# Second rotary attention of an eight-block decoder kernel: who expands the keys, and where its first queries and scores stand

## The chip, the cores and the metric

The kernel is one program on one core of a Trainium2 chip. The metric is the device time in microseconds of one execution, the median of several. The core's engines work from queues of their own: TensorE (PE) for matrix products, VectorE (DVE), ScalarE (ACT), GpSimd (POOL) for elementwise work, and SyncE (SP), which here issues the transfers. They wait for each other by semaphores that the program counts by hand. Fp32 products take two passes over TensorE, so a product of 128x128 by 128x512 appears as two matmuls. TensorE's clock is granted at 1.2 or 2.4 GHz; the profile gives the granted share (PEclk, 1.00 is 2.4 GHz).

## What is computed

x has 16 sequences of 64 tokens with 128 features (1024 tokens). Four pairs of blocks are added to it, each block behind a layer norm and scaled by tanh of a gate:

```
x = x + tanh(g_xattn[0]) * L0_xattn(layernorm(x), ctx)        # a running sum with decay
x = x + tanh(g_ffn[0])   * L0_ffn(layernorm(x))               # 8 experts, 512 hidden
x = x + tanh(g_xattn[1]) * L1_xattn(layernorm(x), ctx)        # first rotary attention
x = x + tanh(g_ffn[1])   * L1_ffn(layernorm(x))               # 8 gated experts, 352 hidden
x = x + tanh(g_xattn[2]) * L2_xattn(layernorm(x), ctx)        # additive attention over all pairs
x = x + tanh(g_ffn[2])   * L2_ffn(layernorm(x))               # 16 gated experts, 128 hidden, top 4
x = x + tanh(g_xattn[3]) * L3_xattn(layernorm(x), ctx, ctx)   # second rotary attention
x = x + tanh(g_ffn[3])   * L3_ffn(layernorm(x))               # 8 + 1 experts, 512 hidden
```

The second rotary attention, which the change is mostly about:

```
Q = (q @ W_q.T).reshape(B, T_q, 16, 8).transpose(0, 2, 1, 3)   # K, V alike from ctx
Q = apply_rope(Q, cos_q, sin_q)
K = apply_rope(K, cos_k, sin_k)
attn = softmax(einsum('bhqd,bhkd->bhqk', Q, K) / sqrt(8))
out = einsum('bhqk,bhkd->bhqd', attn, V) @ W_o.T
```

## The kernel before

All activations lie transposed: features on the 128 partitions, the 1024 tokens as columns in two halves, t = 0 and 1. The program has one function per engine; within it every block is written in the order in which the engine is to do it. What follows are the names that the change and the prediction use.

**Layer norms** have a number j (0 to 7, two per pair of blocks) and a half t. TensorE makes the centred x (`norm_mean`, L442), ScalarE squares it (`norm_square`, L872) and copies it to `xc` (`norm_copy`, L875), TensorE sums the squares (`norm_var`, L449, matmuls with one column), VectorE adds epsilon (`norm_eps`, L1191), GpSimd takes the power -1/2 (`norm_power`, L1688), TensorE spreads it over the partitions (`norm_spread`, L459), and VectorE multiplies (`norm_out`, L1196). `LNBANK` names the PSUM banks of mean, variance and spread. In the MoE blocks `norm_high` and `norm_low` split the result in two for products of three passes.

**Pair sums** (additive attention). For each of 32 groups g VectorE (even g) or GpSimd (odd g) adds features and text to a tile of 2048 columns, ScalarE takes its tanh (L1025) and TensorE sums it with weights (L651). Between the groups stands work for the next block, chosen by `if g == ...` on each engine: norm 5 of the first half, and the key products of the second rotary attention (`prepare_keys`, L490).

**Third MoE** (m.layer 2, 16 experts, 32 steps; step s is expert s % 16 of half s // 16). For each step TensorE makes the two up products (L695 to L697), ScalarE applies silu (`hidden`, L1055), VectorE multiplies both (`product`, L1468, called by `ahead()`), VectorE scales by the token's gate (`scale`, L1476 for steps 0 to 3 with the gate from PSUM, L1480 later with the gate from `g_half`), and TensorE adds the down product (`down`, L712, a plain fp32 product). Up products run 14 steps ahead of down products, so behind step 17 only down products are left. The routing of each half (top experts, weights) is a row of small VectorE instructions, with `ahead()` and norm steps put between them by the lists `first` and `second`. The up weights are split in high and low parts by ScalarE (L920) and GpSimd (`low_up2`, L1704). The down weights of experts 0 to 7 lie in `work[:, 2T:3T]`.

**Rotary attention** (i = 0 and 1) works on 8 pairs of sequences p. `queries(t)` makes two products (L526, L527) from the norm's output; VectorE rotates them (`rotate`, L1208 to L1210) and writes the rows masked for one half of the heads (L1230), ScalarE those of the other (L960). The keys stand rotated in `kT` and are expanded with a mask to 4 copies in `kexp`, which is `work[:, 0:4T]` (`expand_keys`, GpSimd, L1709, four instructions, the last two after the third MoE's step 23, because the down weights lie in their place). Then `scores(p)` (L544), VectorE's maximum and subtraction (`soft`, L1236 and L1240), ScalarE's exponential (L969), TensorE's transposes (`turn`, L554), ScalarE's copies (L978), the values product (L569), VectorE's division (L1248, L1251), `turn_out` and `project`. The first values product writes banks in which the second half's queries stand, and waits for their rotation.

SyncE loads weights into `w_f32`, which has two slots of 1024 columns for the last MoE; each load waits until the split parts of the weights that lay there are made.

## Time and profile before

| | us |
|---|---|
| runs of the kernel | 623.39, 623.45, 624.53 |
| median | 623.45 |
| the profiled execution | 623.69 |
| its span, first to last instruction | 621.9 |
| mean granted clock of TensorE | 0.98 |
| busy: TensorE, VectorE, ScalarE, GpSimd | 568.1, 452.2, 410.7, 125.8 |

The profile is of one execution. Its times count from the first instruction; the 1.8 us between span and execution lie around it. The blocks follow each other: pair sums to 359 us, third MoE to 468, second rotary attention to 510, last MoE to the end. An engine's timeline gives start, duration, engine, source line, operation, output and inputs; the bracket at the end is the idle time in front of the instruction and what ended it. A matmul row's duration can be longer than its share of the engine, since matmuls are pipelined: the distance between starts tells the price. The view of the chain follows the work that ended last back through the engines.

### The profile page before, as it was taken

The page shows a single profiled execution, that of the slowest core. Times are in us where ns is not written, and L with a number is a line of the kernel's source. Part 1 is how long each engine was busy: PE and PEld are TensorE (multiplying, and loading weights), DVE is VectorE, ACT ScalarE, POOL GpSimd, SP SyncE. Part 2 cuts the span into 40 slices and gives each one's busy share as a digit, 9 for nine tenths or more (in the row PEclk, how much of TensorE's full clock was granted, in tenths as well). Part 3 has the DMA queues.
Part 4 walks back from the last instruction along what each step waited for, and adds up shares of the span by engine and source line. Part 5 has one row for each costly group of instructions (what it writes and reads, how often), then busy time and mean ns, then how long its engine had stood idle before and what let it go on. Part 6 is the DMA issues. An engine that isn't in the chain of part 4 may idle for free.

```text
span 621.9 us, 8752 instructions
## 1 busy us (share of the span) xinstructions
PE 568.1 (91%) x3282; PEld 393.1 (63%) x3282; DVE 452.2 (73%) x684; ACT 410.7 (66%) x573; POOL 125.8 (20%) x78
## 2 busy tenths in 40 slices
PE   7999999989998999997866889899978999999997
PEld 5667887747676777774211357466535767688886
DVE  4358988778565898887878486756677946687786
ACT  4779888828654566657999875422303765988885
POOL 5400000332200000005999622200060210000000
PEclk9999999989998999998999899999998999999999
DMA  6217210101102521020000040605600110721100
...
DMA packets 16782, 40.27 MB, mean 65 GB/s; under 512 B 1834, under 2 KB 6058, under 8 KB 16740
## 3 DMA queue, kind: packets, MB, share of 16 engines
...
HBM read 39.01 MB, written 0.70 MB: 64 GB/s over the span
## 4 chain that ended last, share of the span: by engine, by line
PE 68%; DVE 16%; ACT 12%; issue 3%; POOL 1%; DVEq 0%; ACTq 0%; POOLq 0%
PE ps L669 38%; ACT work L1025 7%; PE ps L712 4%; DVE h_lo L1491 3%; PE ps L569 2%; PE ps L695 2%; PE ps L442 2%; PE ps L544 2%; PE ps L697 2%; PE ps L696 2%; PE ps L459 2%; PE ps L449 2%; PE ps L554 1%; PE ps L651 1%; PE ps L436 1%
## 5 line engine op out<-in xcount | busy, mean ns | idle before, releaser
L1491 DVE TENSOR_TENSOR h_lo<-h_act,h_hi 128x512 fp32r<-128x512 f32 (+1 forms) x136 | 120.0, 886 | 41.0 <-ACT h_hi L1062 40.4
L669 PE MATMUL ps<-n_hi,w_hi 128*128 128x512 f32 (+1 forms) x232 | 86.2, 405 | 6.8 <-DVE h_act L1468 4.3
L1062 ACT CAST h_hi<-h_act 128x1024 fp32r<-128x1024 f32 (+1 forms) x88 | 75.3, 856 | 15.3 <-PE ps L669 12.8
L669 PE MATMUL ps<-n_hi,w_lo 128*128 128x512 f32 (+1 forms) x232 | 83.6, 394 | 0.0
L669 PE MATMUL ps<-n_lo,w_hi 128*128 128x512 f32 (+1 forms) x232 | 83.3, 393 | 0.0
L1688 POOL TENSOR_TENSOR rstd<-var_eps,minus_half 128x4 f32<-128x4 f32 x16 | 17.8, 1114 | 315.0 <-DVE var_eps L1191 315.0
L669 PE MATMUL ps<-h_hi,w_hi 128*128 128x512 f32 (+1 forms) x184 | 65.9, 400 | 4.5 <-DVE h_lo L1491 4.3
L669 PE MATMUL ps<-h_hi,w_lo 128*128 128x512 f32 (+1 forms) x184 | 64.5, 393 | 0.0
L669 PE MATMUL ps<-h_lo,w_hi 128*128 128x512 f32 (+1 forms) x184 | 64.4, 392 | 0.0
L1025 ACT ACTIVATE work<-work,p_rest 128x2048 f32<-128x2048 f32 x32 | 61.5, 2000 | 2.0 <-DVE work L1356 2.0
L1722 POOL TENSOR_TENSOR work<-xc,txt 128x2048 f32<-128x2048 f32 x16 | 58.3, 3683 | 5.0 <-ACT xc L1002 4.3
L1055 ACT ACTIVATE h_act<-ps 128x512 f32<-128x512 f32 (+1 forms) x48 | 28.6, 596 | 41.2 <-PE ps L669 41.2
L651 PE MATMUL ps<-work,p_rest 128*32 128x512 f32 x256 | 37.0, 637 | 20.1 <-ACT work L1025 20.1
L669 PEld LDWEIGHTS ps<-n_hi,w_hi 128*128 128x128 f32 (+1 forms) x232 | 42.7, 185 | 19.9 <-DVE h_act L1468 5.4
L669 PEld LDWEIGHTS ps<-n_hi,w_lo 128*128 128x128 f32 (+1 forms) x232 | 42.9, 185 | 10.6
L669 PEld LDWEIGHTS ps<-n_lo,w_hi 128*128 128x128 f32 (+1 forms) x232 | 43.1, 186 | 10.1 <-issue 0.5
L1468 DVE SCALAR_TENSOR_TENSOR h_act<-ps,h_act 128x512 f32<-128x512 f32 (+1 forms) x48 | 32.9, 686 | 20.6 <-ACT h_act L1055 20.5
L669 PEld LDWEIGHTS ps<-h_hi,w_hi 128*128 128x128 f32 (+1 forms) x184 | 34.5, 189 | 15.5 <-DVE h_lo L1491 8.0
L1048 ACT ACTIVATE h_act<-ps,p_attn 128x512 f32<-128x512 f32 (+1 forms) x44 | 38.7, 880 | 4.9 <-PE ps L669 4.4
L1356 DVE TENSOR_TENSOR work<-ps,txt 128x2048 f32<-128x2048 f32 x16 | 36.3, 2282 | 7.3 <-ACT xc L1002 5.2
L1048 ACT ACTIVATE h_act<-ps 128x1024 f32<-128x1024 f32 (+1 forms) x44 | 38.1, 866 | 4.5 <-PE ps L669 4.5
L669 PEld LDWEIGHTS ps<-h_hi,w_lo 128*128 128x128 f32 (+1 forms) x184 | 34.8, 189 | 7.6
...
## 6 DMA issues: line engine op xcount, KB each, us to landing
...
```

What stands on the lines that cost most here:

```text
L651: mm = pe.matmul(ps[32 * q:32 * q + 32, DOTS[g // B]], l2pad[:, 31 - g:63 - g], pairs[:, g % 6, q * 512:(q + 1) * 512], start=(g % B == 0) ...
L669: mm = pe.matmul(dst[i], wap(wt, e, lo, size, rows), mv[i], start=(first and c == 0), stop=(last and c == 2))
L712: pe.matmul(ps[:, acc + t], down2(e), h_part[step % 16], start=False, stop=(step + 1 == m.last_of(t))).then_inc(s["h_used"], 1)
L1025: act.activation(pairs[:, g % 6], pairs[:, g % 6], ACT.Tanh, bias=l2b[:, 0:1]).then_inc(x2["tanh"], 1)
L1048: act.activation(places(h_act, m, step), src, ACT.Gelu, **kw).then_inc(s["act"], 1)
L1055: act.activation(h_part[step % parts][0:size], ps[0:size, 2 * (step % 2)], ACT.Silu, **kw).then_inc(s["act"], 1)
L1062: act.copy(places(h_hi, m, step), places(h_act, m, step)).then_inc(s["hi"], 1)
L1356: dve.tensor_tensor(*sum_of(g, ps[:, FEAT[g // B]]), ALU.add).then_inc(x2["sumA"], 1)
L1468: dve.scalar_tensor_tensor(h, ps[0:size, 2 * sl + 1], b3, h, ALU.add, ALU.mult).then_inc(s["mul"], 1)
L1491: dve.tensor_tensor(lo, src, hi.bitcast(F32), ALU.subtract).then_inc(s["lo"], 1)
L1688: pool.tensor_tensor(rstd[:, r], var_eps[:, r], minus_half[:, r], ALU.pow).then_inc(ln["rstd"], 1)
L1722: pool.tensor_tensor(*sum_of(g, xc[:, half(g // B)]), ALU.add).then_inc(x2["sumB"], 1)
```

## The change

It has five parts.

1. The keys of the second rotary attention are expanded by ScalarE instead of GpSimd, in eight activations of 128x8x64, two behind each of the steps 23, 24, 28 and 29 of the third MoE. GpSimd expands only the keys of the first. The down weights 0 to 7 move from `work` to the second half of `w_f32`, so that `kexp`'s place is free; SyncE loads them once the low parts of the up weights 0 to 7 are made, and the last MoE's second load waits for step 23's down product.
2. The second attention's queries of the first half are made behind down product 28, rotated before the MoE's last sum into x; its first scores stand directly behind the last down product, with the second half's norm around scores 0 and 1.
3. In both attentions the second half's queries stand behind the transposes of pair 0. Norm 2's and 6's second half use banks 6 and 7.
4. In the third MoE `norm_out(5, 1)` is followed by a product, and scale 0 and 1 stand inside the second half's routing.
5. Norm 5's first half is moved by one sum in the pair sums.

The diff, with what the prediction speaks of:

```diff
-        LNBANK.update({(5, 1): (5, 7, 5), (6, 0): (6, 7, 6), (6, 1): (5, 7, 5)})
+        LNBANK.update({(5, 1): (5, 7, 5), (2, 1): (6, 7, 6), (6, 0): (6, 7, 6), (6, 1): (6, 7, 6)})
...
-            return cols(work[:, 2 * T:3 * T] if e < 8 else diag, e, P)
+            return cols(w_f32[:, 8 * P:16 * P] if e < 8 else diag, e, P)
...
                     load_up2(2)
-                    load_down2(0)
                     load_up2(3)
                     sp.wait_ge(x2["bc"], 4)
                     load_down2(1)
+                    low_ready(sp, m, 7, "u")
+                    load_down2(0)
...
                 for e in range(m.slots):
+                    if m.layer == 3 and e == 1:
+                        sp.wait_ge(mo[2]["h_used"], MOES[2].index(7, 1)[0] + 1)
                     load(m, e)
...
+                if i == 0:
+                    queries(0, 0)
+                    norm_mean(2, 1)
+                    norm_var(2, 1)
+                    scores(0, 0)
+                    norm_spread(2, 1)
+                    scores(0, 1)
+                else:
+                    scores(1, 0)
+                    norm_mean(6, 1)
+                    scores(1, 1)
+                    norm_var(6, 1)
+                    keep_busy(2, 4)
+                    norm_spread(6, 1)
                 for p in range(PAIRS):
                     turn(p)
+                    if p == 0:
+                        queries(i, 1)
                     if p + 2 < PAIRS:
-                        scores(p + 2)
+                        scores(i, p + 2)
...
-                    if g in (26, 28):
-                        prepare_keys(1, 0, (g - 26) // 2)
-                    if g == 29:
+                    if g in (26, 29):
+                        prepare_keys(1, 0, (g - 26) // 3)
+                    if g == 28:
                         norm_var(5, 0)
-                    if g == 31:
+                    if g == 30:
                         norm_spread(5, 0)
...
-            moe(MOES[2], {19: [lambda: norm_mean(6, 0)], 21: [lambda: norm_var(6, 0)], 24: [lambda: norm_spread(6, 0)]})
+            moe(MOES[2], {19: [lambda: norm_mean(6, 0)], 21: [lambda: norm_var(6, 0)], 24: [lambda: norm_spread(6, 0)], 28: [lambda: queries(1, 0)]})
...
+            def expand_keys(t, h):
+
+                act.wait_ge(pre["k"], 2 + t + 1)
+                low_ready(act, MOES[2], 15, "u")
+                src = kT[1][:, half(t)].rearrange("p (b k) -> p b k", k=S)
+                ins = act.activation(kexp[:, 8 * t:8 * t + 8, h], src, ACT.Copy, scale=hmask[:, h:h + 1])
+                if h == 3:
+                    ins.then_inc(at["kexp"], 2)
...
-                    if g == 29:
+                    if g == 28:
                         norm_square(5, 0)
                         norm_copy(5, 0)
...
+                        for t in range(2):
+                            if step - 23 - 5 * t in (0, 1):
+                                for h in range(2):
+                                    expand_keys(t, 2 * (step - 23 - 5 * t) + h)
                     load_table(ACT.Exp)
                     norm_square(6, 0)
                     norm_copy(6, 0)
+                    query_rows(1, 0)
                     return
...
+                if i == 0:
+                    query_rows(0, 0)
+                    norm_eps(2, 1)
+                    soft(0)
+                    norm_out(2, 1)
+                    soft(1)
+                else:
+                    soft(0)
+                    norm_eps(6, 1)
+                    soft(1)
+                    norm_out(6, 1)
+                query_rows(i, 1)
...
-                    first = iter([ahead, rest, lambda: norm_eps(5, 1), ahead, rest, lambda: norm_out(5, 1), lambda: norm_low(5, 1), ahead])
+                    first = iter([ahead, rest, lambda: norm_eps(5, 1), ahead, rest, lambda: (norm_out(5, 1), ahead()), lambda: norm_low(5, 1), ahead])
...
-                    for _ in range(3):
+                    for _ in range(2):
                         ahead()
-                    second = iter(6 * [ahead] + 2 * [rest])
+                    second = iter(4 * [ahead] + [lambda t=t: (ahead(), scale(t)) for t in range(2)] + 2 * [rest])
...
+                    query_rows(1, 0)
                     add(1)
                     return
...
-            pool.wait_ge(pre["k"], 4)
-            for q in range(2):
-                expand_keys(1, q)
-            pool.wait_ge(mo[2]["h_used"], MOES[2].index(7, 1)[0] + 1)
-            for q in range(2, 4):
-                expand_keys(1, q)
             norm_power(6, 1)
```

How it moves instructions on the engines. TensorE from the third MoE's last down products (outputs from `vblk`) to the second attention's transposes and first values product, before and, with the line numbers of the changed kernel, after:

```order
L712 MATMUL ps<-vblk,diag 128x512 x4
L526 MATMUL ps<-n,p_rest 128x512
L527 MATMUL ps<-n,p_rest 128x512
L442 MATMUL ps<-x,p_first 128x512
L449 MATMUL ps<-var_w,sq 128x1 x4
L544 MATMUL ps<-work 64x256 x8
L459 MATMUL ps<-p_first,rstd 128x128 x4
L544 MATMUL ps<-work 64x256 x8
L526 MATMUL ps<-n,p_rest 128x512
L527 MATMUL ps<-n,p_rest 128x512
L554 MATMUL ps<-p_first,y_g 128x128 x8
```

```order
L723 MATMUL ps<-vblk,diag 128x512
L528 MATMUL ps<-n,p_rest 128x512
L529 MATMUL ps<-n,p_rest 128x512
L723 MATMUL ps<-vblk,diag 128x512 x3
L544 MATMUL ps<-work 64x256 x8
L445 MATMUL ps<-x,p_first 128x512
L544 MATMUL ps<-work 64x256 x8
L452 MATMUL ps<-var_w,sq 128x1 x4
L439 MATMUL ps<-warm 128x512 x2
L462 MATMUL ps<-p_first,rstd 128x128 x4
L558 MATMUL ps<-p_first,y_g 128x128 x8
L528 MATMUL ps<-n,p_rest 128x512
```

The first half's queries (outputs from n) moved in front of three down products, the scores (from `work`) in front of the mean (from x), and the second half's queries behind the transposes (from `y_g`).

ScalarE in the third MoE's second half, from the activations of steps 20 to 23 (`y_g`) to the table load behind step 31:

```order
L1055 ACTIVATE y_g<-ps,p_rest 128x512 x4
L1055 ACTIVATE txt<-ps,p_rest 128x512 x2
L1055 ACTIVATE kT<-ps,p_rest 128x512 x2
L1055 ACTIVATE vblk<-ps,p_rest 128x512 x4
L892 ACT_TABLE_LOAD
```

```order
L1076 ACTIVATE y_g<-ps,p_rest 128x512 x4
L965 ACTIVATE work<-kT,p_attn 128x8x64 x2
L1076 ACTIVATE txt<-ps,p_rest 128x512
L965 ACTIVATE work<-kT,p_attn 128x8x64 x2
L1076 ACTIVATE txt<-ps,p_rest 128x512
L1076 ACTIVATE kT<-ps,p_rest 128x512 x2
L1076 ACTIVATE vblk<-ps,p_rest 128x512
L965 ACTIVATE work<-kT,p_attn 128x8x64 x2
L1076 ACTIVATE vblk<-ps,p_rest 128x512
L965 ACTIVATE work<-kT,p_attn 128x8x64 x2
L1076 ACTIVATE vblk<-ps,p_rest 128x512 x2
L903 ACT_TABLE_LOAD
```

Four pairs of expansions (into `work`) stand between the activations.

VectorE at the end of the second half's routing in the third MoE (`rt_` tiles), with products (L1468, then L1500) and scalings (L1476, then L1508):

```order
L1376 SCALAR_TENSOR_TENSOR rt_equal<-rt_rank,rt_equal 128x64
L1377 TENSOR_TENSOR rt_chosen<-rt_above,rt_equal 128x64
L1418 TENSOR_TENSOR rt_w<-rt_e,rt_chosen 128x64
L1421 TENSOR_REDUCE rt_m<-rt_w 128x4
L1422 RECIPROCAL rt_m<-rt_m 128x4
L1424 TENSOR_SCALAR rt_m<-rt_m,p_first 128x4
L1425 TENSOR_TENSOR rt_w<-rt_w,rt_m 128x64
L1476 TENSOR_TENSOR h_act<-h_act,ps 128x512 x2
L1468 SCALAR_TENSOR_TENSOR vblk<-ps,p_rest,vblk 128x512
```

```order
L1508 TENSOR_TENSOR h_act<-h_act,ps 128x512
L1408 SCALAR_TENSOR_TENSOR rt_equal<-rt_rank,rt_equal 128x64
L1409 TENSOR_TENSOR rt_chosen<-rt_above,rt_equal 128x64
L1450 TENSOR_TENSOR rt_w<-rt_e,rt_chosen 128x64
L1453 TENSOR_REDUCE rt_m<-rt_w 128x4
L1454 RECIPROCAL rt_m<-rt_m 128x4
L1456 TENSOR_SCALAR rt_m<-rt_m,p_first 128x4
L1457 TENSOR_TENSOR rt_w<-rt_w,rt_m 128x64
L1500 SCALAR_TENSOR_TENSOR vblk<-ps,p_rest,vblk 128x512
```

The two scalings behind the routing are gone from there; the second of them is the first row of the piece after.

## Rows read from the trace of the kernel before

**Rows 1.** the page's busy times, first line: busy us, share, instructions

```profile
PE 568.1 (91%) x3282; PEld 393.1 (63%) x3282; DVE 452.2 (73%) x684; ACT 410.7 (66%) x573; POOL 125.8 (20%) x78
```

**Rows 2.** timeline of the last pair sums: start, us, engine, line, operation, idle before

```profile
350.11 5.79 ACT L1025 ACTIVATE work<-work,p_rest 128x2048 f32<-128x2048 f32 x3
...
350.31 1.05 PE L449 MATMUL ps<-var_w,sq 128*128 128x1 f32 x8
...
352.17 1.06 PE L651 MATMUL ps<-work,p_rest 128*32 128x512 f32 x8 [0.81 <-ACT work L1025]
...
355.81 2.02 PE L459 MATMUL ps<-p_first,rstd 128*128 128x128 f32 x8
...
357.76 1.06 PE L651 MATMUL ps<-work,p_rest 128*32 128x512 f32 x8
```

**Rows 3.** timeline of the first routing in the third MoE

```profile
381.99 0.75 DVE L1468 SCALAR_TENSOR_TENSOR y_g<-ps,p_rest,y_g 128x512 f32<-128x512 f32 x1
...
382.89 0.47 PE L695 MATMUL ps<-n_hi,w_hi 128*128 128x512 f32 x1 [1.35 <-DVE y_g L1468]
...
384.35 0.60 PE L736 MATMUL ps<-p_first,rt_w 128*16 128x128 f32 x4
```

**Rows 4.** timeline of the second routing's end and the first down product

```profile
401.85 1.28 DVE L1476 TENSOR_TENSOR h_act<-h_act,ps 128x512 f32<-128x512 f32 x2
...
402.67 1.10 PE L712 MATMUL ps<-h_act,work 128*128 128x512 f32 x2 [2.12 <-DVE h_act L1476]
```

**Rows 5.** timeline of the last down products and GpSimd's expansion

```profile
447.45 1.12 PE L712 MATMUL ps<-h_act,work 128*128 128x512 f32 x2 [0.45 <-DVE h_act L1480]
...
453.59 9.02 POOL L1709 TENSOR_TENSOR work<-kT,p_attn 128x1024 f32<-128x1024 f32 x4
...
453.87 2.38 DVE L1480 TENSOR_TENSOR kT<-kT,work 128x512 f32<-128x512 f32 x1
...
456.18 0.67 DVE L1196 TENSOR_TENSOR n<-xc,ps 128x512 f32<-128x512 f32 x1
...
458.48 5.88 DVE L1480 TENSOR_TENSOR vblk<-vblk,work 128x512 f32<-128x512 f32 x4
...
463.21 4.54 PE L712 MATMUL ps<-vblk,diag 128*128 128x512 f32 x6 [1.17 <-DVE vblk L1480]
```

**Rows 6.** one line's instructions, 400 to 468 us: ns min/median/max, first and last start

```profile
L1480 DVE TENSOR_TENSOR y_g<-y_g,work x8: 681/684/693, 411.3 to 452.1; 128x512 f32<-128x512 f32 x8
```

**Rows 7.** timeline: ScalarE's last activation there, and its query copy

```profile
445.33 0.69 ACT L1055 ACTIVATE vblk<-ps,p_rest 128x512 f32<-128x512 f32 x1 [1.55 <-PE ps L697]
...
471.56 0.72 ACT L960 ACTIVATE work<-xc,p_attn 128x512 f32<-128x512 f32 x1
```

**Rows 8.** windows: PE, PEld, DVE, ACT, POOL busy, then PEclk

```profile
463.00:468.00 5.00, 4.79 (x7) 2.03 (x8) 1.57 (x4) 0.00 (x0) 0.00 (x0) 0.66 0.00 0
473.00:478.00 5.00, 5.00 (x37) 2.84 (x29) 3.83 (x4) 1.06 (x1) 0.35 (x1) 0.66 0.01 3
```

**Rows 9.** the chain that ended last, 444 to 484 us: start, us, engine, line

```profile
467.75 0.86 PE ps L526 x2
...
472.38 1.09 PE ps L544 x16
...
477.21 1.24 DVE mx L1236
...
478.47 1.22 DVE work L1240
...
480.93 0.70 DVE xc L1210
```

**Rows 10.** timeline: where the second attention's first values product starts

```profile
481.72 1.11 PE L569 MATMUL ps<-vblk,g_sb 128*64 128x18 f32 x32 [0.76 <-issue]
```

**Rows 11.** timeline of the first attention: first transposes, second half's query rotation

```profile
138.69 1.04 PE L554 MATMUL ps<-p_first,y_g 128*128 128x128 f32 x8
...
139.13 0.74 DVE L1208 SCALAR_TENSOR_TENSOR xc<-ps,p_attn 128x512 f32<-128x512 f32 x1
```

91 lines of the change are left out of this document (40 added, 51 removed).

## The prediction

> **What bounds the kernel now.** I read the page's busy times first: TensorE works for 568.1 of 621.9 us [rows 1], so time can be won only where TensorE pauses or runs at half clock, and a step moved on another engine pays only if TensorE waits for it. The waits of TensorE between 340 and 484 us then give four places. (a) The pair sums end with a norm's variance, spread and last sum in a row, though ScalarE's last tanh is over at 355.90 [rows 2]. (b) The first half's routing holds back one product [rows 3]. (c) The first down product waits 2.12 us for the gate scaling behind the second routing [rows 4]. (d) The last down products wait for VectorE, whose scalings stretch while GpSimd expands the keys [rows 5], and behind them stands the start of the second attention [rows 9, 10]. Everywhere between (c) and (d) TensorE is dense, and the rest of the second attention and the last MoE follow (d) unchanged, so what is won here should arrive at the end whole.
>
> The sum is made against the profiled execution, 623.69 us (span 621.9 and 1.8 outside it). That is 0.24 above the median of the runs, 623.45.
>
> **(a) Norm of the third MoE's first half.** Moved: variance before sum 28 instead of 29, spread before sum 30 instead of 31, the second key product into the gap, ScalarE's square and copy ahead of its tanh 28. ScalarE: the same instructions in another order; tanh 31 still ends near 355.9 [rows 2]. VectorE's and GpSimd's rstd then follow VectorE's sum 30 and GpSimd's sum 31 as now, and are ready some 2 us before the spread needs them. TensorE's last sum now ends at 357.76+1.06=358.82, because the spread (2.02) sits between tanh 31 and it. After: the spread fills the wait before sum 30, and sum 31 starts some 0.1 us behind tanh 31, at 356.0, and ends near 357.1. Gain 358.8-357.1 = **1.7**, which both the softmax on VectorE and the copies on ScalarE pass on. Low end 0.3: if the half clock, under which the spread took 2.02 for 8 small matmuls, comes now too, the filled gap is slower by the same amount. High end 2.0. I take 1.7, since the key product now fills the stretch in which TensorE twice waited 0.8 us.
>
> **(b) Product 4 pulled ahead of norm_low.** TensorE waited 1.35 us for it [rows 3]. Without that wait it stands at the transposition of the gates, for which VectorE needs the same steps as before; that now starts at 384.35. VectorE does the same instructions up to the gates, in another order and without idling, so the gates come hardly earlier, at about 384.0. Gain 1.35 at first, **0.35** behind the gates; ends 0 and 1.0.
>
> **(c) Scale 0 and 1 inside the second routing.** scale 0 now runs behind product 12, near 399.4, so the first down product no longer waits: **2.1** [rows 4]. Cost: 2 x 0.64 us (1.28 for two) more VectorE time before the gates of the second half and product 14, which starts near 403.4 instead of 403.0. The up product that needs it starts three pieces of TensorE work later, after 405, so nothing waits. Ends 1.5 and 2.2.
>
> **(d1) Keys expanded by ScalarE.** GpSimd's four expansions take 9.02 us. In exactly that stretch VectorE's scalings (both inputs in SBUF) take 2.38 and on average 5.88/4=1.47 us, where the same line elsewhere has a median of 0.684 [rows 5, 6]; a norm multiplication that reads PSUM stays at 0.67 in the same stretch. So it is GpSimd that stretches them. Without it the tail is TensorE's own: from 447.45 on 13 down products of 0.86, the norm's mean 0.86 and spread 0.86, variance about 0.8, two query products of 0.86 (price in [rows 9]): 17 x 0.86 + 0.8 = 15.4, plus 0.4 of small waits which the stretch up to 456.4 already had, so the last down product ends at 463.3 with the queries already done, against 467.7 now without them [rows 5]. This includes the end of the half clock of [rows 8], in which the last three down products took 4.54 instead of 2.6.
> ScalarE pays: 8 activations of 512 elements a partition, two behind each of steps 23, 24, 28 and 29. It has 1.55 us idle before each activation there; nearest price is the query copy, also from SBUF with a mask as scale, 0.72 [rows 7]. 2 x 0.72 = 1.44 < 1.55: free. The far bound is the slowest 512-element instruction of that stretch, VectorE's 2.38 [rows 5]; at that they would not be free (rival R4). I take 0.72, the same engine and the same form.
>
> **(d2) Start of the second attention.** Queries of the first half run between down products, so VectorE's rotation (three of 0.70) starts at about 460.9 and its mask copy (0.5) ends at 463.4, just as the last down product ends. Scores 0 at 463.7 for 1.09; softmax pair 0 of 1.24 + 1.22 ends at 467.4 [rows 9]; softmax pair 1 beside the second half's variance, rstd and spread until 470.1; norm_out 0.67 until 470.9; transposes of pair 0 done meanwhile; queries 1.72; rotation 2.1; first values product at 475.1. Now it starts at 481.72 [rows 10]. Gain **6.6** for d1 and d2 together at full clock. What pauses again: TensorE waits about 0.5, 1.1 and 1.2 us in this start, and two stretches with such pauses before were followed by half clock (0.66 on average over 463 to 468 and 473 to 478, [rows 8]). I count one such stretch: of the spread and the second half's queries, 0.86+1.72 us of work, about half is doubled, which takes **1.2** back. So d = 5.4; ends 4.0 and 6.8.
>
> **(e) First attention.** The same function puts the second half's queries behind the first transposes. Here nothing else is won: the queries, which ran from 136.9, now wait for the exponential of pair 0 (to 137.3) and the transposes of 1.04 us, so they come 1.4 us later. VectorE, busy with softmax pair 1 until 139.1, hides 0.3 of that; its rotation starts near 140.2 instead of 139.13 [rows 11], and pair 2's softmax and the first output stand behind it. **1.0 lost**; ends 1.3 and 0. The other bank for that half's norm costs nothing: mean and spread share a bank before and after.
>
> **(f) At no cost.** The down weights 0 to 7 go to a free slot of w_f32 after GpSimd's eighth low part (about 373 us) instead of at 359, are needed at 400. On SP the slot makes the last MoE's second load wait for step 23's down product (about 453); behind it on SP stand only loads that wait for splits after 488, and ScalarE reads that slot near 490. If that cover is gone, it would be the transfer's 4 us.
>
> Sum: -1.7 -0.35 -2.1 -5.4 +1.0 = -8.55. 623.69 - 8.55 = 615.1; in the median's frame 614.9, rounded to **615.0**.
>
> **Rivals.** R1: no half clock in the new start; +1.2 won: 613.8. For it: the first attention has the same pauses and kept full clock. R2: half clock also at the end of the pair sums; 1.4 less: 616.4. For it: TensorE works no more there than now. R1 and R2 differ only in the clock. The trace shows it fall to 1.2 GHz after short pauses with work between them. The Trainium skill (TensorE: Matmul & The Clock Gate, HAM oscillation) also tells of kernels where micro-idles alone make the clock swing; by it R2 is the case. R3: the expansion does not stretch the scalings, something else there does; then the tail stays as now and d keeps only the moved queries, about 2: 618.5. Against it: the same line is never slow outside. R4, slower: ScalarE's expansions hold up the up products of the third MoE. ScalarE has 2.25 us a step with 0.69 of its own and TensorE some 1.2 us of slack; each of four steps with two expansions of X delays by 2X+0.69-2.25. At 2.38 each that is 4 x 3.2 - 2.4 = 10.4 lost: 625.4. It decides against the change from X near 2.15, where the loss reaches 8.5. Against it: the 0.72 of [rows 7].
>
> **Chances.** Forecast (614.3 to 615.9) 0.45; R1 0.20; R2 0.16; R3 or another half of d missing 0.10; R4 0.04; a small wait not seen, up to 2 us, 0.05. The range 612.2 to 618.5 leaves out R4, the end of R3, and the sum of all high ends. A measurement of this kernel can tell about 0.2% from no change. Faster by over that: 0.94; same 0.02; slower 0.04.
>
> **What would show it.** (a) last pair sum ends under 1.3 us behind the last tanh. (c) No wait before the first down product. (d) No scaling over 0.8 us; From the start of the down product that waits 0.45 us for its scaling (447.45 now) the last one ends after 15.8 us instead of 20.3, the first scores start within 0.6 us of that, and the first values product starts after 27.7 us (28.9 with one half clock) instead of 34.3. (e) Values product 0 of the first attention 1 us later. Half clock in other stretches than assumed, or ScalarE late at step 24 or 29, would make it wrong.

## The result, and the profile after

The changed kernel takes **614.03 us** (median of four runs, 613.25 to 616.97); the kernel before, run beside it, 623.87 us (623.39 to 624.53). The ratio is 0.9843, with a 95% interval of 0.9804 to 0.9881: faster by 1.6%. The forecast was 615.0, the range 612.2 to 618.5. The profiled execution of the changed kernel took 613.41 us, its span is 611.6 (before 623.69 and 621.9), and its mean granted clock is 0.988 (before 0.980).

The page of the changed kernel, busy times; beside [rows 1] TensorE works 4.6 us less and its pauses are 5.7 us shorter:

```profile
PE 563.5 (92%) x3281; PEld 390.9 (64%) x3284; DVE 445.4 (73%) x684; ACT 415.8 (68%) x581; POOL 117.0 (19%) x74
```

The stretch that the change is about. TensorE of the changed kernel from the last down products on (start, duration, then engine, line, operation, tiles, count, and in brackets the wait and who ended it):

```profile
443.61 1.13 PE L723 MATMUL ps<-h_act,w_f 128*128 128x512 f32 x2 [0.45 <-DVE h_act L1512]
...
455.10 1.02 PE L528 MATMUL ps<-n,p_rest 128*128 128x512 f32 x2
455.96 1.02 PE L529 MATMUL ps<-n,p_rest 128*128 128x512 f32 x2
456.82 2.74 PE L723 MATMUL ps<-vblk,diag 128*128 128x512 f32 x6
459.89 1.09 PE L544 MATMUL ps<-work 64*64 64x256 f32 x16 [0.34 <-DVE work L1253]
...
465.39 1.16 PE L462 MATMUL ps<-p_first,rstd 128*128 128x128 f32 x8 [0.89 <-POOL rstd L1721]
...
467.33 1.12 PE L528 MATMUL ps<-n,p_rest 128*128 128x512 f32 x2
...
471.47 1.11 PE L573 MATMUL ps<-vblk,g_sb 128*64 128x18 f32 x32 [1.14 <-issue]
```

The down product at 443.61 is the one of [rows 5] that stood at 447.45. From it to the end of the last down product it is now 15.8 us (456.82 and three times 0.86 make 459.4), with the queries L528 and L529 of the first half already among them; before it was 20.3. The first scores L544 start at 459.89, 0.5 us behind that end and after a wait of 0.34, and the first values product L573 starts 27.9 us behind the down product at 443.61; in [rows 10] it was 34.3. No half clock is left in this piece (columns: window, its length, busy time of each engine, then the granted clock ahead of the DMA share; [rows 8] are the windows of before):

```profile
456.00:465.00 9.00, 8.09 (x52) 3.72 (x51) 6.52 (x9) 2.85 (x4) 0.67 (x1) 1.00 0.01 2
465.00:474.00 9.00, 7.47 (x84) 5.25 (x88) 6.79 (x9) 3.54 (x6) 0.34 (x1) 1.00 0.00 0
```

VectorE's gate scalings are now all alike; the minimum, median and maximum stand in ns, and the line is L1512. In [rows 5] the one on kT took 2.38 us and those on vblk 1.47:

```profile
L1512 DVE TENSOR_TENSOR vblk<-vblk,work x8: 678/682/686, 427.2 to 454.9; 128x512 f32<-128x512 f32 x8
...
L1512 DVE TENSOR_TENSOR kT<-kT,work x4: 681/683/686, 421.4 to 452.5; 128x512 f32<-128x512 f32 x4
```

ScalarE's expansions, two at a time (L965), between its activations L1076. Two take 1.32 us together, and 0.34 us are left before the next activation, where [rows 7] had 1.55:

```profile
424.10 1.32 ACT L965 ACTIVATE work<-kT,p_attn 128x512 f32<-128x512 f32 x2
425.76 0.69 ACT L1076 ACTIVATE txt<-ps,p_rest 128x512 f32<-128x512 f32 x1 [0.34 <-PE ps L708]
```

The end of the pair sums, TensorE. The last sum ends at 358.04, 2.0 us behind ScalarE's last tanh (356.01); in [rows 2] it ended at 358.82, 2.9 us behind it:

```profile
351.56 2.08 PE L493 MATMUL ps<-ctxT,p_rest 128*128 128x512 f32 x2
353.56 1.54 PE L662 MATMUL ps<-work,p_rest 128*32 128x512 f32 x8
355.04 1.16 PE L462 MATMUL ps<-p_first,rstd 128*128 128x128 f32 x8
356.12 1.92 PE L662 MATMUL ps<-work,p_rest 128*32 128x512 f32 x16
```

and the start of the first attention, where the values product L573 stood at 141.31 before:

```profile
132.73 1.98 PE L544 MATMUL ps<-work 64*64 64x256 f32 x16 [0.44 <-DVE work L1253]
134.64 1.85 PE L462 MATMUL ps<-p_first,rstd 128*128 128x128 f32 x8
...
139.32 1.02 PE L528 MATMUL ps<-n,p_attn 128*128 128x512 f32 x2
...
143.44 1.11 PE L573 MATMUL ps<-vblk,g_sb 128*64 128x18 f32 x32 [1.21 <-DVE xc L1236]
```

One thing stands in the trace of the kernel before too, and the prediction overlooked it: a stretch of half clock at 125 to 129 us, at the start of its first attention. The first row has the matmuls of one query line in it (minimum, median and maximum in ns, first and last start): the slowest took 1061 ns where 592 is the price at full clock. The second is a window (columns as above), with a granted clock of 0.66:

```profile
L526 PE MATMUL ps<-n,p_attn x4: 592/876/1061, 126.4 to 137.4; 128*128 128x512 f32 x4
```

```profile
125.00:130.00 5.00, 4.79 (x9) 2.35 (x9) 2.61 (x5) 0.00 (x0) 0.00 (x0) 0.66 0.00 0
```

**The span in seven pieces.** To see where the 10.3 us of the span went, and to compare kernels whose executions differ in their half-clock stretches, the table cuts every profiled span at six places: A up to the first queries of the first attention, B up to the gates' transposition of the second MoE, C up to the first pair sum, D up to the last matmul of the pair sums, E up to the first down product of the third MoE, F up to the last one, G up to the end. The edges are the first and last starts of those lines; for the changed kernel they are read from these rows and from the transposition at 194.8, in the view of a line's instructions (the last two numbers of a row are the first and the last start in us):

```profile
L528 PE MATMUL ps<-n,p_attn x4: 592/825/1061, 126.3 to 139.8; 128*128 128x512 f32 x4
```

```profile
L662 PE MATMUL ps<-work,p_rest x256: 592/617/1063, 292.4 to 357.5; 128*32 128x512 f32 x128
```

```profile
L723 PE MATMUL ps<-h_act,w_f x16: 590/591/697, 398.9 to 444.1; 128*128 128x512 f32 x16
...
L723 PE MATMUL ps<-vblk,diag x16: 590/592/595, 430.1 to 459.0; 128*128 128x512 f32 x16
```

A star stands for a stretch of half clock that began in the piece or up to 3 us ahead of it (two stars: two of them, or one of double length); one behind the last matmul of a span is left out. "f" marks a piece with useless matmuls in TensorE's waits, "q" a piece F that holds the two queries, 1.7 us, which stand in G otherwise.

| kernel | A | B | C | D | E | F | G | span |
|---|---|---|---|---|---|---|---|---|
| before | 126.4 | 66.3* | 99.1* | 66.4*** | 44.5 | 64.5* | 154.7* | 621.9 |
| changed | 126.3 | 68.5** | 97.6 | 65.1** | 41.4 | 60.1q | 152.6 | 611.6 |
| GpSimd's keys | 128.1* | 67.2* | 100.4** | 66.0**** | 41.5 | 64.6q* | 154.2* | 622.0 |
| second start old | 128.1* | 67.2* | 100.5** | 66.1**** | 41.4 | 58.4 | 154.6* | 616.3 |
| first start old | 125.5 | 65.8* | 99.1* | 65.8*** | 41.5 | 60.1q | 152.6 | 610.4 |
| norm old | 126.3 | 68.4** | 97.6 | 65.9** | 41.5 | 60.1q | 154.1* | 613.9 |
| lists old | 128.1* | 67.2* | 100.4** | 66.0**** | 45.9* | 61.8q* | 152.6 | 622.0 |
| expansions twice | 126.3 | 67.1* | 100.3** | 66.0**** | 41.5 | 64.5q* | 154.1* | 619.8 |
| both starts old | 126.4 | 66.1* | 99.2* | 65.5*** | 41.5 | 58.3 | 154.8* | 611.8 |
| same, filled first | 125.4 | 65.4f | 97.7f | 65.0f | 41.5 | 58.3 | 154.1f | 607.4 |
| same, filled anew | 125.4 | 65.0f | 97.6f | 63.8f | 41.4 | 58.4 | 154.0f | 605.6 |
| same, long waits filled | 127.6* | 65.7f* | 97.6f | 64.7f* | 41.5 | 58.3 | 154.8* | 610.2 |
| before, filled | 127.6* | 65.0f | 97.7f | 65.9f* | 44.4 | 64.5* | 154.0f | 619.1 |
| changed, filled | 125.4 | 67.3f* | 97.7f | 63.7f | 42.5* | 60.1q | 152.7 | 609.4 |

The table shows the size of one half-clock stretch by pieces that hold the same work: in C, a dense MoE, 1.5 us for one and 2.8 for two; in E and F 1.1 to 1.7; in B 0.7 to 1.4; in G, 0.6 to 0.8 in the old start (154.6 to 154.8 against 154.0), whose waits take up half of it, and 1.5 in the new one (154.1 against 152.6). The 2.2 us in A (127.6 against 125.4) are not the stretch alone: in the filled kernel before, 1.3 of them are lost in the first 8.2 us, ahead of it. From before to after the pieces give 0.1, -2.2, +1.5, +1.3, +3.1, +4.4 and +2.1 us, together the 10.3 of the span. Pieces B to D differ from what the change was costed at there: B has a stretch more, C and D have one less each.

### The profile page after: what moved, and what is told of

It is laid out like the page before. It is cut to its first block, busy times and chain, and to the rows that moved or that the text cites. A ratio compares the mean times of both kernels' runs of the same rounds, so it can differ in the third digit from the quotient of the medians.

```text
span 611.6 us, 8766 instructions
## 1 busy us (share of the span) xinstructions
PE 563.5 (92%) x3281; PEld 390.9 (64%) x3284; DVE 445.4 (73%) x684; ACT 415.8 (68%) x581; POOL 117.0 (19%) x74
## 4 chain that ended last, share of the span: by engine, by line
PE 71%; DVE 13%; ACT 11%; issue 3%; POOL 1%; ACTq 0%; DVEq 0%; POOLq 0%
PE ps L680 38%; ACT work L1046 7%; PE ps L723 4%; DVE h_lo L1523 3%; PE ps L445 2%; PE ps L573 2%; PE ps L706 2%; PE ps L544 2%; PE ps L708 2%; PE ps L707 2%; PE ps L462 2%; PE ps L662 2%; PE ps L558 2%; PE ps L452 2%; PE ps L439 1%
## 5 line engine op out<-in xcount | busy, mean ns | idle before, releaser
L1755 POOL TENSOR_TENSOR work<-xc,txt 128x2048 f32<-128x2048 f32 x16 | 58.3, 3684 | 5.0 <-ACT xc L1023 4.3
L1076 ACT ACTIVATE h_act<-ps 128x512 f32<-128x512 f32 (+1 forms) x48 | 28.6, 596 | 39.6 <-PE ps L680 39.6
L1500 DVE SCALAR_TENSOR_TENSOR h_act<-ps,h_act 128x512 f32<-128x512 f32 (+1 forms) x48 | 32.9, 685 | 19.1 <-ACT h_act L1076 19.0
L680 PEld LDWEIGHTS ps<-h_hi,w_hi 128*128 128x128 f32 (+1 forms) x184 | 34.3, 188 | 15.4 <-DVE h_lo L1523 7.8
```

What stands on the lines that cost most here:

```text
L680: mm = pe.matmul(dst[i], wap(wt, e, lo, size, rows), mv[i], start=(first and c == 0), stop=(last and c == 2))
L1076: act.activation(h_part[step % parts][0:size], ps[0:size, 2 * (step % 2)], ACT.Silu, **kw).then_inc(s["act"], 1)
L1500: dve.scalar_tensor_tensor(h, ps[0:size, 2 * sl + 1], b3, h, ALU.add, ALU.mult).then_inc(s["mul"], 1)
L1755: pool.tensor_tensor(*sum_of(g, xc[:, half(g // B)]), ALU.add).then_inc(x2["sumB"], 1)
```

## The experiments

Each starts from the changed kernel unless it says otherwise. The diffs are cut to their core.

**Keys expanded by GpSimd.**

```diff
-                        for t in range(2):
-                            if step - 23 - 5 * t in (0, 1):
-                                for h in range(2):
-                                    expand_keys(t, 2 * (step - 23 - 5 * t) + h)
...
             norm_power(6, 0)
+            pool.wait_ge(pre["k"], 4)
+            for q in range(4):
+                expand_keys(q, 1)
             norm_power(6, 1)
```

> The changed kernel with one thing put back: the keys of the second attention are expanded by GpSimd (four of 1024 elements, some 9 us in a row), not by ScalarE. My theory: GpSimd's expansions stretch VectorE's gate scalings, which TensorE then waits for. So the scalings beside them take 1.2 to 1.6 us instead of 0.68, the stretch from the start of the down product that waits 0.4 us for its scaling to the end of the last down product goes from 15.8 to 17.5 to 19 us, and the whole time is 2 to 3.5 us longer than that of the changed kernel: about 616.8. Rival: something else in the old order stretched them (the queries' place, the half clock), and then the scalings stay at 0.7, the stretch at 15.8 to 16.1, and the time within 0.4 us of the changed kernel's.

The times were 618.17 to 624.02 us, median 622.22, ratio to the kernel before 0.9963 (0.9938 to 0.9989). GpSimd of this kernel, and beside it VectorE's scalings (L1508) and TensorE's down products (L723):

```profile
453.98 9.02 POOL L1738 TENSOR_TENSOR work<-kT,p_attn 128x1024 f32<-128x1024 f32 x4
```

```profile
452.45 0.69 DVE L1508 TENSOR_TENSOR y_g<-y_g,work 128x512 f32<-128x512 f32 x1
...
454.27 2.38 DVE L1508 TENSOR_TENSOR kT<-kT,work 128x512 f32<-128x512 f32 x1
456.57 0.67 DVE L1218 TENSOR_TENSOR n<-xc,ps 128x512 f32<-128x512 f32 x1
...
458.87 5.88 DVE L1508 TENSOR_TENSOR vblk<-vblk,work 128x512 f32<-128x512 f32 x4
```

```profile
459.00 1.12 PE L723 MATMUL ps<-kT,diag 128*128 128x512 f32 x2 [1.17 <-DVE kT L1508]
461.30 1.99 PE L723 MATMUL ps<-vblk,diag 128*128 128x512 f32 x2 [1.18 <-DVE vblk L1508]
```

Before GpSimd starts, a scaling takes 0.69 us; during its 9.02 us the first on kT takes 2.38 and those on vblk 1.47 each, while the norm's product L1218, which reads one operand from PSUM, stays at 0.67. Undoing this one edit brings the stretching back, and with it two waits of 1.2 us. Piece F is 4.5 us longer than in the changed kernel, where 1.7 to 3.2 were expected: 2.35 are the two waits, some 1.7 a half-clock stretch behind them, which was not expected, and 0.4 is not put down to anything. The first theory holds, and the rival (the scalings stay at 0.7) falls. This is also the rule of the Trainium skill, "SBUF — State Buffer", Who interferes with whom: a VectorE instruction with both inputs in SBUF contends with a GpSimd instruction that reads SBUF, one with a single SBUF input, outside the two-port modes, does not. The trace agrees in both halves: 1.47 to 2.38 us and 0.67. The median stands further off than 616.8, because this kernel's executions had clocks down to 0.972; its fastest run, 618.17 at clock 0.981, is 3.5 above the changed kernel's run at that clock, 614.66.

**Old start of the second attention, keys still by ScalarE.**

```diff
+                    queries(1, 0)
-                    scores(1, 0)
                     norm_mean(6, 1)
-                    scores(1, 1)
                     norm_var(6, 1)
-                    keep_busy(2, 4)
+                    scores(1, 0)
                     norm_spread(6, 1)
+                    scores(1, 1)
+                    queries(1, 1)
...
-moe(MOES[2], {..., 28: [lambda: queries(1, 0)]})
+moe(MOES[2], {...})
```

The queries thus leave the down products and the place behind the first transposes; VectorE and ScalarE follow in the same order, and the norm is back in its old banks.

> The changed kernel with the old start of the second attention (queries of both halves behind the last down product and ahead of the first transposes, variance ahead of the first scores), keys still expanded by ScalarE. Prediction's own split (the moved queries alone are worth about 2 us): the first values product 0 starts 29.8 us behind the waiting down product instead of 27.9, time about 616. Rival, worked out anew from the trace of before: the last down product ends 1.7 us earlier, since the queries are not among them (14.1 instead of 15.8), and from there it took 14.0 us to the first values product against 12.1 now, so the whole stretch is 28.1 at the same clock and 26.9 if the half clock does not come: the new start is then worth nearly nothing, 0.2 us, and the time is 613.4 to 614.3.

Median 613.67 us (613.26 to 618.09), ratio 0.9859 (0.9821 to 0.9897): level with the changed kernel. The last down products and the start in the profiled execution:

```profile
448.03 1.12 PE L724 MATMUL ps<-h_act,w_f 128*128 128x512 f32 x2 [0.44 <-DVE h_act L1512]
...
462.10 1.02 PE L528 MATMUL ps<-n,p_rest 128*128 128x512 f32 x2
...
466.90 1.09 PE L544 MATMUL ps<-work 64*64 64x256 f32 x16 [0.31 <-DVE work L1252]
467.92 1.67 PE L462 MATMUL ps<-p_first,rstd 128*128 128x128 f32 x8
469.52 1.99 PE L544 MATMUL ps<-work 64*64 64x256 f32 x16
...
476.09 1.11 PE L573 MATMUL ps<-vblk,g_sb 128*64 128x18 f32 x32 [0.60 <-issue]
```

From 448.03 to the values product at 476.09 are 28.06 us, 0.2 more than in the changed kernel, with a half-clock stretch inside (the spread L462 took 1.67 and the scores 1.99). The prediction's own split, 2 us for the moved queries, falls. Pieces F and G together are 213.0 us here and 212.7 in the changed kernel; without the stretch the old start gives 212.4 (filled kernel, below). So the **moved queries and scores are worth between -0.3 and +0.3 us**: what they win ahead of the first scores (4.8 us from the end of the last down product to the scores here, 0.5 in the changed kernel) they lose twice, as 1.7 us of queries that now lengthen the down products, and as 2.4 us more between the scores and the values product (11.6 against 9.2), since the second half's queries and rotation now come behind the transposes. With GpSimd's keys the new start looks a little better: F and G are 218.8 with the new start and 219.2 and 218.5 with the old one, though a stretch in G costs the new start 0.7 us more (1.5 against 0.8). The new start has two of the waits of 1.2 us there, the old one three: the moved queries stand in the place of the third.

**Old order in the first attention.**

```diff
-        LNBANK.update({(5, 1): (5, 7, 5), (2, 1): (6, 7, 6), (6, 0): ...
+        LNBANK.update({(5, 1): (5, 7, 5), (6, 0): ...
                     norm_spread(2, 1)
                     scores(0, 1)
+                    queries(0, 1)
                 for p in range(PAIRS):
                     turn(p)
-                    if p == 0:
+                    if p == 0 and i:
                         queries(i, 1)
```

> The changed kernel with the old order in the first attention only (second half's queries ahead of the first transposes, its norm back in the old banks). Theory: the order costs 1.0 us and the other 1.1 us, by which the changed kernel was later at its first values product (143.44 against 141.31), were a half-clock stretch that comes or not. So at full clock the product stands at 141.3 to 141.5, with such a stretch at 142.4 or so, and the total is 1.0 us less than the changed kernel's where the other stretches have the same clock: about 613.0. Rival: the new order itself calls the half clock, and the old one is free of it in every look: 2.1 less. Second rival: what is won here is given back before the third MoE, as the half clock wanders to a later stretch: no change in total.

Median 613.00 us (612.12 to 614.50), ratio 0.9834 (0.9810 to 0.9859). The values product stands at 139.91, 14.4 us behind the first queries at 125.5, against 17.1 in the changed kernel; the spread shows the half-clock stretch of this execution:

```profile
131.46 2.07 PE L462 MATMUL ps<-p_first,rstd 128*128 128x128 f32 x8
...
139.91 1.11 PE L573 MATMUL ps<-vblk,g_sb 128*64 128x18 f32 x32 [0.85 <-DVE xc L1237]
```

The expected places, 141.3 at full clock and 142.4 with a stretch, are missed: they were taken from two traces that both had the stretch at 125 us, and this one has it at 131. Piece B tells order and clock apart. The old order gives 65.0 to 65.4 (filled) without a stretch and 65.7 to 66.3 with one; the new one 67.1 to 67.3 with one and 68.4 to 68.5 with two. With one stretch, at the same place (124 to 129 us), it is 66.1 and 66.3 against 67.1 and 67.2: the new order costs **about 1.0 us**, and a stretch 0.7 to 1.3. The first rival falls, since the old order has a stretch too. The second is not excluded: of the 3.5 us that this execution wins in A and B, 2.2 are gone again in C and D, where two stretches more stand, and the median is only 1.0 us under the changed kernel's, with intervals that overlap.

**Old order at the end of the pair sums.**

```diff
-                    if g in (26, 29):
-                        prepare_keys(1, 0, (g - 26) // 3)
-                    if g == 28:
+                    if g in (26, 28):
+                        prepare_keys(1, 0, (g - 26) // 2)
+                    if g == 29:
                         norm_var(5, 0)
-                    if g == 30:
+                    if g == 31:
                         norm_spread(5, 0)
...
-                    if g == 28:
+                    if g == 29:
                         norm_square(5, 0)
                         norm_copy(5, 0)
```

> The changed kernel with the old order at the end of the pair sums (variance of the third MoE's norm ahead of sum 29, spread ahead of sum 31, second keys product ahead of sum 28). Theory: 0.85 us later there, as the two traces showed with a half-clock stretch in each (last sum ends 2.9 us behind the last tanh instead of 2.1), and all of it arrives: about 614.9. If the half clock does not come, the difference is 1.7, as predicted. Rival: routing behind it, which hangs on VectorE and not on TensorE, hides it: the first waiting product of the first routing stands at the same place, no change in the total.

Median 615.57 us (615.13 to 618.08), ratio 0.9881 (0.9855 to 0.9908). Its end of the sums, where ScalarE's last tanh ends at 355.94:

```profile
355.65 2.08 PE L462 MATMUL ps<-p_first,rstd 128*128 128x128 f32 x8
357.66 1.16 PE L662 MATMUL ps<-work,p_rest 128*32 128x512 f32 x8
```

The last sum ends 2.9 us behind the last tanh, as in [rows 2], and piece D is 65.9 against 65.1, both with two stretches; piece E is the same, so the routing behind it hides nothing. The moved norm is worth **0.8 us** where the half clock comes into both orders; what it is worth with none in either, no run shows. The profiled span is 2.3 longer; the other 1.5 are a stretch in piece G.

**VectorE's old lists.**

```diff
-... rest, lambda: (norm_out(5, 1), ahead()), lambda: norm_low(5, 1), ahead])
+... rest, lambda: norm_out(5, 1), lambda: norm_low(5, 1), ahead])
-                    for _ in range(2):
+                    for _ in range(3):
                         ahead()
-                    second = iter(4 * [ahead] + [lambda t=t: (ahead(), scale(t)) for t in range(2)] + 2 * [rest])
+                    second = iter(6 * [ahead] + 2 * [rest])
...
-                    for step in range(2, m.total):
-                        if step + 12 < m.total:
+                    for step in range(m.total):
+                        if step >= 2 and step + 12 < m.total:
```

> The changed kernel with the old routing lists of VectorE in the third MoE (product 4 behind the norm's low part, gate scalings 0 and 1 behind the second routing). Theory: TensorE waits 1.3 us again for a product in the first routing and 2.1 us before the first down product, and from the last pair sum's end to the down product that waits 0.4 us it takes 3.0 us more (0.6 for the first list, 2.4 for the second). At the same number of half-clock stretches the time is 3.0 us above the changed kernel's: 617 as median. Rival: the 2.1 us were VectorE's and return as a wait a few products later, so that the difference is under 1.5 us.

Median 622.09 us (619.69 to 624.87), ratio 0.9963 (0.9938 to 0.9988). Waits of TensorE in its pieces E and the first down products (us in total, times, longest):

```profile
PE ps L723 <- DVE h_act L1508: 2.1, 1, 2.1
PE ps L706 <- DVE y_g L1500: 1.3, 1, 1.3
```

Both waits are back. Piece E is 45.9 us with a stretch of half clock at 386 to 390 in dense products (1.5 by the rate of piece C), so 44.4; without stretches it is 44.5 in the kernel before and 41.4 in the changed one. So **the lists are worth 3.0 us**, and the rival (VectorE gives the 2.1 us back later) falls: piece F is 61.8 with a stretch against 60.1. The median of this kernel again holds more half clock than the edit explains (its clocks are 0.972 to 0.983, those of the changed kernel 0.974 to 0.988).

**Each expansion done twice on ScalarE.**

```diff
+                act.activation(kexp[:, 8 * t:8 * t + 8, h], src, ACT.Copy, scale=hmask[:, h:h + 1]).then_inc(again, 1)
+                act.wait_ge(again, 4 * t + h + 1)
                 ins = act.activation(kexp[:, 8 * t:8 * t + 8, h], src, ACT.Copy, scale=hmask[:, h:h + 1])
```

> The changed kernel with each of ScalarE's eight expansions of the keys done twice (the second waits for the first): four of some 0.7 us behind each of four steps instead of two. By the prediction's price of such a delay (rival R4): a step then holds 2.65 us or a little more of expansions and 0.69 of its own activation against a period of 2.25 us, so ScalarE falls 1.1 to 1.3 us behind in each of four steps; with 1.2 us of slack for each pair of steps TensorE loses 2.0 to 2.8 us: about 616.5. Rival: TensorE is further ahead than 1.2 us (four products stand in front of each), and loses nothing: within 0.4 us of the changed kernel.

Median 621.80 us (615.68 to 623.80), ratio 0.9945 (0.9912 to 0.9977). ScalarE at steps 28 and 29, and the waits of TensorE:

```profile
438.56 0.71 ACT L966 ACTIVATE work<-kT,p_attn 128x512 f32<-128x512 f32 x1
439.30 0.72 ACT L968 ACTIVATE work<-kT,p_attn 128x512 f32<-128x512 f32 x1
...
441.30 0.67 ACT L1079 ACTIVATE vblk<-ps,p_rest 128x512 f32<-128x512 f32 x1
```

```profile
PE ps L724 <- DVE h_act L1515: 2.0, 2, 1.2
PE ps L707 <- DVE txt L1503: 0.7, 1, 0.7
```

Four expansions take 2.8 us. Piece F is 64.5 us with one stretch of half clock against 60.1, so 2.7 to 2.9 us are lost, at the top of the expected 2.0 to 2.8, and the rival (nothing lost) falls. The waits name most of it: 2.7 us, of which 0.45 were there before. A step of ScalarE takes 3.3 us here (441.30 less 438.56, and 0.57 of its own) against the period of 2.25, so two steps in a row put it 2.1 us behind, and TensorE waits 0.7 us for the first pair: the **slack is about 1.4 us**. The changed kernel, with 0.34 us idle in each of these steps, does not touch it; expansions of over 0.83 us each would begin to.

**Both starts old**, the edits of the second and the third experiment together (one line of each):

```diff
+                    queries(0, 1)
...
+                    queries(1, 1)
```

> The changed kernel with the old start in both attentions; kept are ScalarE's keys, the moved norm and the two lists of VectorE. The traces so far, at the same number of half-clock stretches, say that the new start costs 1.4 us in the second attention (168.0 us from the waiting down product to the end, against 168.3 with one such stretch of 1.7 in the old start) and 1.0 us in the first. By that this kernel is 2.4 us faster than the changed one where the stretches are equally many, about 611.8 as median if they are. Rival: the old starts, with their shorter and denser waits in another order, catch more half-clock stretches (one more, 1.7 us), and the median is level with the changed kernel's, 613.3.

Median 612.95 us (612.50 to 613.68), ratio 0.9817 (0.9799 to 0.9836), that is 1.1 us under the changed kernel's median, with intervals that overlap. The expected 611.8 was too low: it priced the stretch in the second start at 1.7 us, and the pieces show 0.8. What is left of the 2.4 us is the first attention's 1.0 and 0.3 of the second's.

**Useless matmuls in TensorE's waits.** The stretches of half clock stood at nearly the same places in every trace, so the next kernels fill the pauses. First, with both starts old:

```diff
-..., 41: [lambda: norm_spread(2, 0)]})
+..., 41: [lambda: norm_spread(2, 0)], 42: [lambda: keep_busy(8, 2)]})
...
                         turn_gates()
+                        if L == 1:
+                            for _ in range(12):
+                                pe.matmul(ps[64:128, 7], warm[:, 0:64], warm[:, :], start=True, stop=True)
...
+                    if g == 0:
+                        keep_busy(16, 1)
...
+                    if g == 2 or 11 <= g < 30:
+                        keep_busy(2, 4)
...
+                    keep_busy(3, 4)
                     norm_var(6, 1)
+                    keep_busy(1, 4)
                     scores(1, 0)
...
+                keep_busy(6 if i == 0 else 2, 4)
                 for p in range(PAIRS):
                     turn(p)
```

keep_busy(count, bank) multiplies bf16 numbers that nothing reads. The first attention has the same lines as the second.

> The kernel of both old starts, and beside it matmuls without a use (bf16, 0.21 us each, on banks of PSUM that are free) where TensorE waits: 8 ahead of the last product of the first MoE, 12 of 64 columns behind the gates' transposition of the second, 16 ahead of the pair sums, 2 ahead of most of the pair sums, 4 to 10 in the starts of the attentions. Theory: the half-clock stretches, of which 4 to 10 stood in each run and each of which takes about 1.7 us, follow stretches in which TensorE pauses; filled, they do not come. At most one remains, the granted clock is 0.995 or more, and the time falls by 6 to 10 us against the kernel without them, to 602 to 606. Rival: the stretches come of something else (heat, a limit on power), and more work gives as many or more: clock 0.98 as before, and the time 0 to 3 us longer.

Median 609.47 us (609.18 to 611.28), ratio 0.9767 (0.9746 to 0.9788). No stretch of half clock stands in the trace of the profiled execution, where the one without the filling had six (one of double length counted twice). One exception does not show in the granted clock: the eight bf16 matmuls at the very start of the kernel take 3.23 us, 0.4 each, where the later ones take 0.21; in the kernel before they take 3.59 us. The theory holds for the clock, the rival (more work, more half clock) falls. The gain is 3.5 us and misses the expected 6 to 10 (602 to 606), since that took each stretch at 1.7 us, which is more than the pieces show, in the pair sums above all, where TensorE waits for ScalarE; and since the fillings of sums 23 to 29 cost TensorE time it did not have (piece D: 65.0, filled, against 63.8 in the next kernel).

**The filling thinned out**, against the kernel just told of:

```diff
-                    if g == 2 or 11 <= g < 30:
+                    if g in (2, 28) or 11 <= g < 23:
                         keep_busy(2, 4)
...
+                    keep_busy(4, 4)
                     queries(1, 1)
-                keep_busy(6 if i == 0 else 2, 4)
```

> The kernel with both old starts, filled as these two (the useless matmuls ahead of pair sums 23 to 31 left out but for 28, those ahead of the first transposes moved ahead of the second half's queries, which waited 1.1 us for their norm). The earlier filling, at clock 1.0, had 609.2 us and lost 1.3 us on the last pair sums, where TensorE had no slack, and 0.4 us ahead of the second attention's transposes. Theory: these come back, 607.4 at clock 0.997 or more, the fastest of all. Rival: with less filling a half-clock stretch comes at the end of the pair sums or in the second start, and the time is level, 609.

Median 609.10 us (607.44 to 611.99), ratio 0.9768 (0.9741 to 0.9795). Two of five runs are at clock 1.000, with 607.44 and 608.06; the others at 0.997. Core, span and clock of the profiled one:

```profile
core 0: 605.6 us, clock 1.000
```

The 1.2 us in piece D came back, and with the two clean runs the 607.4 of the theory; the median is level with the first filling's, as the clock was 0.997 in three of five runs. These two are the fastest kernels of the study.

**Only the three long waits filled**, that is this kernel without the filling of single sums and of the starts:

```diff
-                    if g in (2, 28) or 11 <= g < 23:
-                        keep_busy(2, 4)
...
-                    keep_busy(3, 4)
                     norm_var(6, 1)
-                    keep_busy(1, 4)
                     scores(1, 0)
```

> The kernel with both old starts and only the three long waits filled (8 ahead of the last product of the first MoE, 12 behind the gates' transposition of the second, 16 ahead of the pair sums). Theory: the stretches at 125, 197 and the first of the two at 289 us follow pauses of 2, 3 and 4.3 us and are gone; those in the midst of the pair sums (335, 351 or 355) and of the second start (463 to 468), where TensorE pauses under 1.4 us again and again, stay. Clock 0.989 to 0.993, time 608.5 to 610. Rival: the long pauses are the only cause, and the clock is 0.998 as in the fully filled one.

Median 610.80 us (608.83 to 611.98), ratio 0.9790 (0.9765 to 0.9814), clocks 0.983 to 0.992, a little behind the expected 608.5 to 610; the rival (clock 0.998) falls. The stretches at 125, 197 and 289 us are gone, those at 11, 133, 348 and 461 us have stayed or come. So long pauses are one cause, and a row of short pauses with sparse work between is another.

**The same filling in the changed kernel and in the kernel before.** These two take the clock out of the comparison as far as it goes. Beside the three long waits and the single sums, the start of the first attention is filled in both, that of the second in the kernel before only (in the changed kernel the last four matmuls stand ahead of the first transposes):

```diff
                 norm_mean((2, 6)[i], 1)
+                keep_busy(3, 4)
                 norm_var((2, 6)[i], 1)
+                keep_busy(1, 4)
                 scores(0)
                 norm_spread((2, 6)[i], 1)
                 scores(1)
+                keep_busy(4, 4)
                 queries(1)
```

> The changed kernel, with useless bf16 matmuls in TensorE's waits: 8 ahead of the last product of the first MoE, 12 (64 columns) behind the gates' transposition of the second, 16 ahead of the pair sums, 2 ahead of pair sums 2, 11 to 22 and 28, 3, 1 and 4 in the start of the first attention. No half clock is expected but at most one stretch, clock 0.997 or more. Set beside the same filling of the kernel before (it should be 6 us slower) and of the kernel with the old starts (it should be 2.4 us faster), it gives what the parts are worth without the half clock: about 609.7. Rival: the new starts cost nothing once the half clock is away, and this kernel is level with the one with the old starts within 0.4 us.

> The kernel before, with the same useless matmuls in the same places, and in both attention starts. Theory: the change is worth 6.0 us without the half clock (0.8 for the moved norm, 0.6 and 2.4 for VectorE's lists, 3.2 for the keys and the new start, less 1.0 for the first attention), and the rest of the 9.6 us measured was half-clock stretches which the changed kernel had fewer of. So this one comes at 615.7 where its clock is 0.995 or more, 1.7 us more for each stretch that is left (the waits of 1.3, 2.1 and 3 us in the third MoE are not filled). Rival: the change is worth 9 us or more at full clock too: 618.7 or more with no stretch left.

The changed kernel filled has a median of 612.04 us (611.16 to 614.92), ratio 0.9828 (0.9798 to 0.9859); the kernel before filled 619.19 (618.88 to 620.91), ratio 0.9933 (0.9911 to 0.9955). They are 7.15 us apart, against 9.84 unfilled. The first expectation is missed: 612.0 for 609.7, as stretches came at 141 (1.3 us in B) and 356 us (1.1 in E), and with them the two kernels cannot decide what the starts are worth; pieces F and G do (212.8 against 212.4). The second expected 615.7 and 1.7 more for each stretch, and the profiled execution (span 619.1) has three, at 10, 352 and 461 us. Less what they cost by the table (2.2 in A, about 1 in D, 1.5 in F) the span is 614.4, and with the 1.8 outside it 616.2; so the rival's 618.7 at full clock falls, by this estimate, since no execution of this kernel was without a stretch. The filled changed kernel, less 1.3 and 1.1, comes to 608.8 in the same way. So by this estimate the change is worth **about 7.4 us with no stretch anywhere**, not 6.0, and the rest of the 9.8 is half clock. The stretch at 461 us stands where nothing was filled, behind the waits that GpSimd's expansions cause:

```profile
458.82 1.12 PE L719 MATMUL ps<-vblk,diag 128*128 128x512 f32 x2 [1.18 <-DVE vblk L1490]
461.12 4.54 PE L719 MATMUL ps<-vblk,diag 128*128 128x512 f32 x6 [1.18 <-DVE vblk L1490]
```

Three down products (six matmuls, 2.74 us in the changed kernel) take 4.54 us there. This stretch is in all three traces with keys by GpSimd (463, 461 and 461 us), always behind two or three waits of 1.2 us. Of the eleven traces with keys by ScalarE one has a stretch in these last down products (449 us), the one in which the expansions were doubled and TensorE waited 1.24 and 0.73 us. So it goes with GpSimd's expansions and is counted as a part of the gain. The other two of the kernel before (197 and the second at 289 us) stand in work that the change does not touch, and are absent from the changed kernel's profile but stand in five of the six traces in which one edit of it was undone or doubled, so their absence is no gain of the change.

## Why the prediction was right, step by step

The sum was -8.55, and the medians are 9.8 apart; the profiled pair 10.3. The four terms together measured 9.3 (0.8 + 3.0 + 6.5 - 1.0) in the profiled pair: (a) came 0.9 short, the others gave 1.7 more, so the hit within 1 us owes something to errors that cancel. Of the cases R1 came true in the new start (no half clock, 613.8 forecast for it) and R2 at the end of the pair sums (a stretch there, 1.4 the other way).

- **(a) The moved norm: 1.7 predicted, 0.8 measured.** The order did what was said: the keys' product and the spread stand in the former waits. The term was mis-sized in its clock: the half clock came there too (keys 2.08 us, sum 29 1.54), the condition named as low end and as R2. By its own sign for this term, a last sum that ends under 1.3 us behind the last tanh, the prediction missed: it ends 2.0 us behind. In the filled kernels, D is 63.7 for the new order without a stretch and 65.9 for the old with one.
- **(b) and (c) The two lists: 0.35 + 2.1 predicted, 3.0 measured.** Right in mechanism. By the positions of the gates' transposition (384.35 before, 382.96 now, less the 0.8 of (a)) 0.6 us of it are (b)'s and 2.4 (c)'s. TensorE waits for nothing ahead of the first down product at 398.91, and the wait for the gates is 0.75.
- **(d) Keys and second start: 5.4 predicted (6.6 without a new stretch), 6.5 measured** as pieces F and G, 219.2 against 212.7. No stretch came in the start. The sum held, its split did not: (d2) was taken to bring the queries and scores forward by 2 us, and that step fails. The second experiment puts d2 at -0.3 to +0.3; the whole gain is d1's, 4.5 us of waits and some 1.5 of a half-clock stretch that GpSimd's expansions bring on; about 0.7 is a stretch of the old start that did not come in the new one. The error came from adding up the new start by itself, and not beside the old start on the same scale: queries included, the way from the last down product's end to the values product is 13.8 us in the new order (12.1 and 1.7) and 14.0 in [rows 9, 10], where a stretch of half clock is among the 14.0.
- **(e) First attention: +1.0 predicted, +1.0 measured**, and in the profiled pair 2.1, as a second stretch came there. The prediction named this start as evidence for R1, since it "has the same pauses and kept full clock". That reading was wrong: half clock stood there before as well, at 125 to 129 us. R1 came true without this reason for it.
- **(f) At no cost: held.** The down weights' move shows nowhere in E and F; no run undoes it by itself.
- **ScalarE's price: 0.72 predicted, 0.66 a piece measured** (1.32 for two), as they overlap a little. **R3** fell (GpSimd's experiment), **R4** did not happen, but its price of a delay was near: 2.0 to 2.8 us expected by it for the doubled expansions, 2.7 to 2.9 measured.
- **Luck in the range.** Piece C, which the change leaves alone, gave 1.5 us back by the clock alone, and the start of D another 0.5 (1.3 less the 0.8 of the norm), against the 1.3 lost in B. A prediction of this kernel cannot be better than such stretches: the changed kernel's four runs alone differ by 3.7 us, with clocks of 0.974 to 0.988. Whether a stretch comes in C, in an execution of the same code, stays open; the filling shows only that it comes of the pause.
